# A block's loads and stores of ternary weights, shared out between the SyncE and the GpSimd DMA queue

## The reference, cut to what matters

```python
def _weight_quant(w):
    scale = 1.0 / jnp.clip(jnp.mean(jnp.abs(w)), 1e-05)
    wq = jnp.clip(jnp.round(w * scale), -1.0, 1.0) / scale
    return w + jax.lax.stop_gradient(wq - w)
...
def _bitlinear(x, w):
    return jnp.einsum('bsi,oi->bso', _act_quant(x), _weight_quant(w))
gate = jax.nn.silu(_bitlinear(x, w_gate))
up = _bitlinear(x, w_up)
return _bitlinear(gate * up, w_down)
...
x = x + _layernorm(_L0_attn_ref(_layernorm(x, axis=-1), ...), axis=-1)
x = x + _layernorm(_L0_ffn_ref(_layernorm(x, axis=-1), w_gate, w_up, w_down), axis=-1)
```

## Time and profile before

| | |
|---|---|
| Median of 3 runs | 4142.91 us (4141.91 to 4145.91) |
| The profiled execution, its own time | 4144.47 us |
| Its span, slowest core (core 2) | 4142.9 us |
| Spans of all cores | 4121.5 to 4142.9 us |
| Busy: PE, DVE, ACT, POOL | 1294.9, 1498.0, 1450.0, 266.2 us |
| DMA, queue of SyncE and ScalarE (q1) | 235.07 MB, 17.3% of 16 engines |
| DMA, queue of GpSimd (q0) | 8.65 MB, 1.4% of 16 engines |
| 1 MB loads of w_gate, w_up, w_down | 32 each, 6.2, 6.4 and 6.0 us from issue to landing (median) |

### The profile page before, as it was taken

The page is one execution under the profiler, slowest core; times in us unless marked ns, Lnnn a source line. Parts: engine busy times, 40 slices in busy tenths (PEclk is TensorE's granted clock), DMA queues, the critical chain, the costliest instruction groups (busy, mean ns, idle before and its releaser), DMA issues.

```text
span 4142.9 us, 25493 instructions; the slowest of 8 cores (4121.5 to 4142.9 us)
## 1 busy us (share of the span) xinstructions
PE 1294.9 (31%) x5181; PEld 530.4 (13%) x5260; DVE 1498.0 (36%) x2016; ACT 1450.0 (35%) x2106; POOL 266.2 (6%) x443
## 2 busy tenths in 40 slices
PE   1122110001110112022743621742621655417453
PEld 0100000000000001000311200311200222103221
DVE  0067756891000001000166982256882141021400
ACT  3644433334444443466123333223343211132201
POOL 0012211230000000000010320000000000000000
PEclk9975555555555556555875655875655876659766
DMA  4000010103225220423410101220101221103111
GB/s 65 0 0 1 0 20 31 61 31 109 94 90 184 95 94 25 171 92 122 137 56 6 55 11 41 86 67 6 51 15 41 83 71 36 45 32 102 51 41 51
DMA packets 164347, 245.36 MB, mean 59 GB/s; under 512 B 6113, under 2 KB 121058, under 8 KB 160098
## 3 DMA queue, kind: packets, MB, share of 16 engines
q1 hardware_dynamic: 159906, 235.07, 17.3%
q0 software_dynamic: 4288, 8.65, 1.4%
HBM read 218.80 MB, written 33.55 MB: 61 GB/s over the span
## 4 chain that ended last, share of the span: by engine, by line
DVE 25%; ACT 22%; PE 21%; DMA 14%; issue 10%; POOL 6%; ACTq 1%; DVEq 1%; SPq 0%; POOLq 0%
DVE s_sig L289 11%; POOL s_state L263 6%; PE pU L845 5%; PE pG L837 5%; PE pD L965 5%; DVE s_sig L296 4%; DMA wu_buf<-wu 4%; DMA wg_buf<-wg 3%; DMA s_td<-tdT 2%; DVE s_ytmp L313 2%; DMA wdn_buf<-wdn 2%; ACT s_h L927 2%; PE ptD L920 2%; PE pW L662 2%; DVE s_qs L869 2%
## 5 line engine op out<-in xcount | busy, mean ns | idle before, releaser
L282 ACT ACTIVATE s_abar<-s_dyq,s_nega 128x512 f32<-128x512 bf16 x512 | 369.4, 722 | 613.0 <-DVE s_sig L289 465.9
L289 DVE TENSOR_TENSOR_SCAN s_sig<-s_abar,s_state,s_lnf 128x512 bf16<-128x512 f32 x384 | 493.0, 1284 | 112.2 <-ACT s_abar L282 67.7
L965 PE MATMUL pD<-s_td,s_h 128*128 128x512 bf16 x1000 | 383.9, 563 | 222.3 <-DMA s_td<-tdT 213.1
L837 PE MATMUL pG<-s_tg,s_dyq 128*128 128x512 bf16 x980 | 382.3, 390 | 115.8 <-DVE s_h L864 115.5
L845 PE MATMUL pU<-s_tu,s_dyq 128*128 128x512 bf16 x1024 | 399.3, 390 | 22.8 <-DMA s_tu<-tuT 16.5
L313 DVE SCALAR_TENSOR_TENSOR s_ytmp<-s_sig,s_bprm,s_ytmp 128x512 bf16<-128x512 bf16 x448 | 336.5, 751 | 48.9 <-DVE s_sig L289 2.3
L263 POOL TENSOR_TENSOR s_state<-s_sig,s_onesp 128x1 bf16<-128x1 bf16 x384 | 247.9, 646 | 1275.9 <-DVE s_sig L296 447.1
L864 DVE TENSOR_TENSOR s_h<-s_gtmp,pU 128x512 bf16<-128x512 bf16 x128 | 88.0, 688 | 656.1 <-ACT s_gtmp L857 656.1
L857 ACT ACTIVATE s_gtmp<-pG,s_r1g 128x512 bf16<-128x512 f32 x128 | 88.0, 687 | 422.7 <-PE pU L845 252.9
L965 PEld LDWEIGHTS pD<-s_td,s_h 128*128 128x128 bf16 x1024 | 133.1, 134 | 472.2 <-issue 456.7
L662 PE MATMUL pW<-s_w,s_dyq 128*128 128x512 bf16 x251 | 90.9, 538 | 324.3 <-DVE s_x L682 198.9
(11 more groups left out here) (156 smaller groups left out, 1736.9 us busy)
## 6 DMA issues: line engine op xcount, KB each, us to landing
wg_buf<-wg SPq DMA_DIRECT2D x32, 1024.0 KB, 6.2
wu_buf<-wu SPq DMA_DIRECT2D x32, 1024.0 KB, 6.4
wdn_buf<-wdn SPq DMA_DIRECT2D x32, 1024.0 KB, 6.0
s_tg<-tgT SPq DMA_DIRECT2D x64, 512.0 KB, 3.6
s_tu<-tuT SPq DMA_DIRECT2D x64, 512.0 KB, 4.7
s_td<-tdT SPq DMA_DIRECT2D x64, 512.0 KB, 3.6
tgT<-wg_stage SPq DMA_DIRECT2D x16, 512.0 KB, 3.5
tuT<-wu_stage SPq DMA_DIRECT2D x16, 512.0 KB, 3.5
```

The lines of the kernel that those rows point to most:

```text
L282: lambda h, d=dc, n_=n, p=pa: h.activation(out=s_abar[:, p, :], in_=delta_view[:, d, t0:t0 + QT], func=AF.Exp, scale=s_nega[:, d, n_:n_ + 1]),
L289: lambda h, d=dc, c_=col, p=pa, s=ps: h.tensor_tensor_scan(s_sig[:, s, :], s_abar[:, p, :], lnT_view[:, d, t0:t0 + QT], s_state[:, c_:c_ + 1],
L837: h.matmul(pGs[c_][:], q1T_view[:, k, t_ * 128:(t_ + 1) * 128], s_tg[:, wp, k4_, :], start=(k == 0), stop=(k == KC - 1)),
L965: lambda h, c_=c, k=kc, p=par, s_=sub, f=hf: h.matmul(pDs[c_][:, f * 512:(f + 1) * 512], q2T_view[:, c_, k, :], s_td[:, p, s_, f * 512:(f ...
```

## The change

Places 0 and 2 of `wbuf` are loaded by SyncE as before, places 1 and 3 by GpSimd, in both passes; the store of `stage` is issued by GpSimd. Waits, sizes, buffers and semaphores stay as they are. So of each weight's 32 loads 16 move (the odd pieces of both passes), and all 36 stores move.

```diff
@@ scale pass
-                sch.dma("sync", f"wbuf{par}",
+                sch.dma("sync" if par % 2 == 0 else "gpsimd", f"wbuf{par}",
                         lambda h, q_=q, p=par: h.dma_start(
                             out=wbuf[:, p, :, :], in_=wv4_slice(q_)),
                         waits=w_dma)
@@ ternary pass
-                                sch.dma("sync", f"wbuf{par4}",
+                                sch.dma("sync" if par4 % 2 == 0 else "gpsimd",
+                                        f"wbuf{par4}",
                                         lambda h, q_=q, p=par4: h.dma_start(
                                             out=wbuf[:, p, :, :], in_=wv4_slice(q_)),
                                         waits=[t_sign[q - RING] if q >= RING
@@ store of a row pair
-                    t_st2 = sch.dma("sync", "stage_st",
+                    t_st2 = sch.dma("gpsimd", "stage_st",
                                     lambda h, rp_=rp: h.dma_start(
                                         out=wTv[:, :, rp_ * 256:(rp_ + 1) * 256], in_=stage[:]),
                                     waits=[t_ev])
```

## The result

The changed kernel takes 4224.6 us (median of 8 runs, 4214.8 to 4233.9), the one before 4145.2 us beside it; the ratio is 1.019, with a 95% interval of 1.0176 to 1.0204. It is slower by 79 us. The forecast was 4277 us, slower by 134, with a range of 4190 to 4410: the direction and the place of the loss were right, its size was two thirds too large.

A forecast was written before the change was run, and what follows sets the result against it. Stages were taken as chains bound by ScalarE's waits, not DMA rate. Scale passes 47.0 + 42.7 + 44.4, ternary passes -8.0 - 0.3, last stores +8.4 gave +134.2 us: 4277 us, range 4190 to 4410.

The forecast's parts named there:

- The scale passes: Scale passes of w_gate, w_up and w_down: odd loads no longer issued ahead, +47.0, +42.7 and +44.4 us.
- the mechanism that was named: Scale passes: GpSimd's list puts the addition of piece q-1 ahead of odd load q, so its whole flight is idle time.
- The lone waits: Scale passes, odd loads alone in flight: each waits 5.7 + 2.0 = 7.7 us instead of 0.55.
- the shared ones: Scale passes, odd loads in flight with a SyncE load released by the same sum: 8.7 us each, 1.0 of it sharing.
- The loss beside the scans: w_gate's scale pass: pieces 1 and 3 add 2.0 us each, 5 and 7 get 6.2 each, +16.4 us.
- the price of the queue: GpSimd's DMAs: 1.8 us later start plus 15 ns a packet; load +2.0 us, small store +2.8, large +5.6.
- The rival of a small price: All moved DMAs: GpSimd's queue costs only 0.4 us each, sum +10, 4153 us; chance 0.04.
- w_down's ternary pass: Three waits behind the 2 MB store change by -0.1 us each, -0.3; with its last store +5.3 us.
- the two rivals and the far end: Outside the range: GpSimd's queue no dearer (4130 us, chance 0.05), price of 0.4 us (4153, 0.04), beyond 4450 (0.04).
- The small store: Ternary passes of w_gate and w_up: a 512 KB store on GpSimd's queue is 2.8 us dearer, landing at 6.4 us.
- The rival of slow 512-byte rows: Stores: GpSimd writes descriptors slowly for 512-byte rows, +114 us, 4391 us; chance 0.26, and 0.04 beyond 4450.
- The odd pieces of the ternary pass: w_gate and w_up: eight odd loads stay behind the stores, now in GpSimd's list, losing 2.0 + 0.5 us each, 20.0.

The follow-up runs named there:

- run with the order alone: Kernel before, all DMAs on SyncE; the scale pass's odd loads from piece RING on also wait for GpSimd's addition of the piece before: ratio 1.0179, 4225 us.

## Why the prediction was right, and where its size was off

*The scale passes* were the large loss, by the mechanism that was named: +111 us measured, +134 predicted. Taking the addition out of the way gives 95 of them back with the queue unchanged; putting the addition in the way costs 71 with no GpSimd DMA at all. Both are shown. The lone waits were put at 7.7 us and measured 6.1 to 6.3; the shared ones at 8.7 and measured mostly 7.6 to 7.9. The split was wrong as well: I took 2.0 for the queue and 1.0 for sharing; the runs show about 0.5 for the queue and 1.5 to 2 for sharing in the changed kernel (7.6 to 7.9 against 6.1 to 6.3; two of w_up's waited 8.9 and 9.2). The loss beside the scans was +16.4 in the sum; the measured 35.1 less the 25.6 of the four waits past the scans leaves 9.5. VectorE's idle time before a scan is 5.0 and 4.4 us where the state save stands behind a GpSimd load; it was 4.21 at piece 1 before, and I had put 6.2.

*The mis-sized term is the price of the queue.* The step read: "Difference 1.3 to 2.4 us; I take 1.8." It was read from converting loads of 1024 rows. A moved load starts 1.4 us after its issue instead of 0.9, so the price is 0.5 us, below the low end of my bounds. The rows that I took belonged to another kind of transfer.

The rival of a small price stood at 0.4 us, with a chance of 0.04; but its sum was +10, and +79 was measured. Its price of the queue was nearly right and its time was not. It kept sharing at 1.0 where the runs show about 2 (some 13 us), it gave the odd pieces of w_gate's and w_up's ternary passes 0.4 us each where they lost 2.1 (27 us; it had even dropped the 0.5 us that the sum allows for GpSimd's longer issue), and it had a gain in w_down's ternary pass where there was a loss (about 21 us). So 4277 came nearer with a wrong price because the price, too high, stood in for costs that the sum left out or had too low; that part is luck.

The Trainium skill's figures for the first byte (DMA: Bandwidth & Descriptors, Latency and other measured facts), about 0.6 and 1 us, differ by 0.4 us. The traces of the moved loads agree with that difference (0.5), though both starts, 0.9 and 1.4 us, come some 0.3 to 0.4 us later than the page has them.

One sum of chances is wrong as it was recorded: the two rivals and the far end that the range leaves out have 0.05, 0.04 and 0.04, which is 0.13 and not 0.09.

*The small store* was put at 2.8 us dearer. It is issued 0.54 us after the last copy's end (1077.36 and 1097.72 show it, against 0.07 in the earlier trace rows) and lands in 3.9 instead of 3.5: 0.9 in all. So the wait for it, 3.1 in the sum, is 1.0 net: 12.9 us in seven waits, and 5.9 us of waits for transposes gone that they cover. That makes 13 us for each of w_gate and w_up. With the odd pieces (below) and, for w_gate, the last store it explains nearly all of -18.9 and -21.2 against -1.2 and -4.0. The packets show where the 15 ns for each 512-byte row are missing. A store of w_gate on GpSimd's queue, in the changed kernel (DMA rate in slices of 0.2 us, then the queue: packets, MB, share):

```profile
GB/s 0 0 0 0 0 0 0 0 184 328 307 246 287 287 287 307 307 82 0 0 0 0 0 0 0 0 0 0 0 0 0 0 0 0 0 0 0 0 0 0
...
q0 software_dynamic: 144, 0.52, 22.0%
```

and one of w_up on SyncE's, before (the same two rows, slices of 0.18 us):

```profile
GB/s 0 0 0 0 0 0 0 0 162 300 280 286 303 286 286 294 297 280 179 3 0 0 0 0 0 0 0 0 0 0 0 0 0 0 0 0 0 0 0 0
...
q1 hardware_dynamic: 1040, 0.52, 24.5%
```

For the same 0.52 MB the one queue moves 144 packets, the other 1040. The rival of slow 512-byte rows fell with it: it wanted over 8 us for such a store.

*The odd pieces of the ternary pass* were to lose 2.5 us and lost 2.1 (9.1 against the 7.0 of the same pieces before). Here the parts were wrong and the sum nearly right, which is luck. The load is issued 1.4 us after the last copy's end (1078.23 after 1076.81) and was issued 0.5 us after it (1065.25): 0.9 us later, by GpSimd's late start and its longer issue of the store. The queue's start gives 0.5. The rest shows as a pause of the engines between the store and the load (changed kernel, slices of 0.3 us from 1077 us):

```profile
GB/s 410 396 410 410 205 0 273 328 259 287 314 232 55 0 0 0 150 14 41 273 164 314 164 273 410 423 423 369 287 150 41 0 0 0 0 0 0 0 0 0
```

The store's bytes end at 1080.9, and for 0.9 us nothing moves, although the load was issued at 1078.23. What causes the pause was not traced.

*w_down's ternary pass* came out at +5.4 for +5.3, and this is luck too. Its store lands in 14.4 us in the median, 4.7 more than on SyncE, where 5.6 were assumed. But that is no price of the queue alone. The last store, with no load beside it, on GpSimd's queue and on SyncE's (KB, us to landing):

```profile
tdT<-wdn_stage POOLq DMA_DIRECT2D x1, 2048.0 KB, 10.7
...
tdT<-wdn_stage SPq DMA_DIRECT2D x1, 2048.0 KB, 9.2
```

So the large store alone is dearer by 1.5 us of flight and 1.0 of late issue, not by 5.6; in the first three row pairs a load of SyncE's starts moving some 9 us after the store's issue and runs beside it. By parts (medians over the cores) the three row pairs behind a store changed by -0.3 us, as predicted, and the last store cost 2.7 us, 2.9 less. The first row pair lost 2.7 us, which the sum had at nothing: piece 1, now loaded by GpSimd, is waited for 8.26 us on the slowest core, against 5.36 before. The two errors cancel.

*The stages left alone*, the start and the matmuls, differ by 3 us of 2800, with the cores 25 us apart among themselves; nothing was traced to the change there.

Why two loads in flight cost the second some 2 us, and not the 3.4 us that 1 MB takes at full rate, can be read in part from the queues at 962 to 969.8 us: the second load's packets start when the first one's are nearly done, and the first had been issued 0.65 us earlier. The run with the order alone fits: there the odd load is the first of the two and waits 5.4 to 6.7 us. What stays open is why the later load is served behind the earlier one and not beside it; no run varied the size or the distance of the two, and for ScalarE's queue, which the trace puts together with SyncE's, the packets can't be told apart. Also open is what delays GpSimd's issue by 0.3 to 0.6 us after what it waits for; the trace calls it "issue".

## What to carry to other kernels

Before moving a DMA to another engine, write down what stands in front of it in both lists. A list that holds loads alone runs ahead by as many buffers as there are, and one instruction that waits for the consumer takes all of it away; here the same move, of a DMA to GpSimd's queue, was worth -4.0% for the stores and cost +2.6% for the odd loads of the scale passes. Share out by kind (loads in one list, stores in another), not by even and odd. Where two lists let go a load each at the same moment, see that the one that is needed first is issued first, as it was in the run with the order alone. And read a queue's price from the transfer nearest in kind, not from the only ones at hand: keep the bound open below when they differ in rows and conversion.

## What the runs showed of the hardware

- The same store of 1024 rows of 512 bytes is 144 packets on GpSimd's queue and 1040 on SyncE's, at much the same rate (most slices above between 280 and 307 GB/s).
- A plain 1 MB load from GpSimd's queue starts 1.4 us after its issue when it is alone (SyncE's 0.9); the converting ones of the same queue started after 2.2 and 3.2 us.
- With another 1 MB load issued just before it, a load's wait goes from mostly 5.4-5.7 to 7.5-8.9 us on hardware queues, from mostly 6.0-6.3 to 7.6-9.2 on GpSimd's. In the pair that is shown, none of the later load's 272 packets (GpSimd's) moved before 966.2 us, 3.4 us after its issue, while 232 of SyncE's did.
- GpSimd is held 0.74 us for the issue of a plain 1 MB load of w_gate and 0.9 us for a 512 KB store, SyncE 0.37 us for either; a DMA on ScalarE delays the next scaling by 0.7 to 1.0 us.
